# Feed layer of a four-stage transformer kernel: the first two attention tiles' scores, maxima and exponentials are issued among the last projected tiles

## The reference, cut to what matters

```
for l in range(2):                      # DEPTH
    h = shift_token(x)                  # 2048 tokens x 128 channels
    q, k, v = split(h @ wqkv)           # 8 heads x 64
    q, k = l2norm(q) * qs, l2norm(k) * ksc
    q, k = rotary_xpos(q, k)
    sim = 8.0 * q @ k                   # windows of 64, each with the one before it
    attn = softmax(where(mask, -max, sim))
    x = x + (attn @ v) @ wo
    h = layernorm(shift_token(x)) * lg + lb
    a, g = split(h @ w1 + b1)
    x = x + (a * gelu(g)) @ w2 + b2
```

## Time and profile before

| | |
|---|---|
| median of 3 runs | 1183.13 us (1181.82 to 1184.08) |
| the profiled execution | 1179.29 us, its span 1177.5 us |
| busy PE, DVE, ACT, POOL | 84%, 65%, 46%, 38% of the span |
| mean granted TensorE clock | 0.916 of full speed |
| feed loop and attention of layer 0 | about 766 to 939 us of the span |
| the same of layer 1 | about 968 to 1141 us of the span |

### The profile page before, as it was taken

How to read it: one execution, slowest core, us unless ns; L and a number is a source line. 1 busy time by engine, 2 the same in 40 slices (tenths; PEclk the granted TensorE clock), 3 DMA queues, 4 the chain that set the end, 5 groups by cost and what they waited for, 6 DMA issues and landing times.

```text
span 1177.5 us, 19933 instructions
## 1 busy us (share of the span) xinstructions
PE 990.9 (84%) x8002; PEld 661.3 (56%) x8002; DVE 762.8 (65%) x1340; ACT 537.3 (46%) x1243; POOL 452.9 (38%) x480
## 2 busy tenths in 40 slices
PE   5986997875479999999998568599698899979987
PEld 4645564744236787887877323245466534456643
DVE  7693585747556674554645888699566549946653
ACT  7745576462245423021120600067686436768632
POOL 7978106142025400000000345379454238934420
PEclk8977889987669999999999789799899999979999
DMA  3306818172428255236521100000121210012201
GB/s 109 73 1 120 148 25 148 26 132 55 166 109 153 45 108 131 53 107 108 94 57 71 60 1 0 0 1 1 37 55 38 72 52 27 1 38 55 56 1 36
DMA packets 60008, 75.58 MB, mean 64 GB/s; under 512 B 37460, under 2 KB 41952, under 8 KB 58188
## 3 DMA queue, kind: packets, MB, share of 16 engines
q1 hardware_dynamic: 59916, 74.31, 28.2%
HBM read 51.82 MB, written 1.51 MB: 45 GB/s over the span
## 4 chain that ended last, share of the span: by engine, by line
PE 56%; DVE 16%; POOL 15%; ACT 6%; issue 5%; DMA 1%; SPq 0%; POOLq 0%; DVEq 0%; ACTq 0%
PE psum L1630 7%; PE psum L1632 7%; PE psum L1631 7%; POOL rest L1909 3%; POOL rest L1899 3%; POOL rest L1905 3%; PE psum L2152 2%; PE psum L2145 2%; ACT rest L1843 2%; PE psum L2198 2%; PE psum L754 2%; POOL rest L1935 2%; DVE main L1999 2%; PE psum L2161 1%; PE psum L834 1%
## 5 line engine op out<-in xcount | busy, mean ns | idle before, releaser
L1843 ACT ACTIVATE rest<-psum,main 128x128 f32<-128x128 f32 x256 | 113.4, 480 | 11.4 <-POOL main L1920 8.9
L1349 POOL TENSOR_TENSOR kept<-kept 128x4 f32<-128x4 f32 x8 | 2.4, 303 | 295.2 <-DVE kept L1364 295.2
L1272 ACT ACTIVATE x_high<-main 128x512 fp32r<-128x512 f32 x48 | 30.4, 633 | 144.0 <-DVE main L1441 144.0
L1935 POOL TENSOR_TENSOR rest<-rest,main 128x512 f32<-128x512 f32 x64 | 65.4, 1044 | 45.5 <-DVE main L2005 45.5
L1630 PE MATMUL psum<-x_high,w_low 128*128 128x512 f32 x192 | 77.2, 402 | 0.7 <-DVE x_low L1446 0.7
L1630 PE MATMUL psum<-hid_high,w_low 128*128 128x512 f32 x192 | 75.8, 395 | 0.8 <-DVE main L1503 0.8
L1632 PE MATMUL psum<-x_high,w_high 128*128 128x512 f32 x192 | 75.8, 395 | 0.0
L1631 PE MATMUL psum<-x_low,w_high 128*128 128x512 f32 x192 | 75.7, 394 | 0.0
L1631 PE MATMUL psum<-hid_low,w_high 128*128 128x512 f32 x192 | 74.9, 390 | 0.0
L1632 PE MATMUL psum<-hid_high,w_high 128*128 128x512 f32 x192 | 74.8, 389 | 0.0
L1999 DVE TENSOR_REDUCE main<-psum 128x4 f32<-128x512 f32 x64 | 41.2, 686 | 40.5 <-PE psum L2145 40.4
(11 more groups left out here) (388 smaller groups left out, 2788.3 us busy)
## 6 DMA issues: line engine op xcount, KB each, us to landing
rest<-share_d SPq DMA_DIRECT2D x4, 3072.0 KB, 21.4
main<-main SPq DMA_DIRECT2D x32, 256.0 KB, 6.3
main<-k_pad SPq DMA_DIRECT2D x16, 512.0 KB, 8.0
rest<-share_d SPq DMA_DIRECT2D x4, 2048.0 KB, 16.9
rest<-main SPq DMA_DIRECT2D x32, 256.0 KB, 3.5
main<-w_dram SPq DMA_DIRECT2D x2, 3072.0 KB, 14.0
main<-rest SPq DMA_DIRECT2D x32, 128.0 KB, 2.3
rest<-tables_dram SPq DMA_DIRECT2D x2, 2048.0 KB, 8.7
```

The lines of the kernel that those rows point to most:

```text
L1843: last = A.activation(probs[:, p, 4 * r + m, :], bank[2 * p + r][:, m * P:(m + 1) * P], ACT.Exp, scale=row_scale[:, c, r, m:m + 1], bias=r ...
L1935: nc.gpsimd.tensor_tensor(probs[:, c % 2, four_heads], probs[:, c % 2, four_heads], row_sum[:, c % 2, four_heads].unsqueeze(2).to_broadcas ...
```

## The change

PE issues `score(0)` in round 16, ahead of the transposes of tile 14, and `score(1)` in round 17, ahead of those of tile 15. It waits there for the banks of tiles 14 and 15 (`ff_rot`, `ff_sq`, `ff_v`) and for the first two tiles of `qhT` and `khT`.

ACT copies the transposes of tile 14 ahead of the last root, takes the exponentials of tile 0 ahead of the copies of tile 15, and those of tile 1 behind them.

DVE takes `maxima(0)` ahead of the last inverse (round 16).

POOL makes `row_scale` of tiles 0 and 1 in round 3, that of the other 14 after the loop, and `bias(0)` ahead of the scaling of k of tile 15.

```
@@ ff_act
-                for c in range(TILES + 2):
+                def turned(c):
+                    for name, dst, bk in (("q", qhT, 4), ("k", khT, 5)):
+                        act.wait_ge(sem(f"ff_{name}T_ps"), L * TILES + c + 1)
+                        A.activation(dst[:, :, c * P:(c + 1) * P], bank[bk][:, :].rearrange("p (j t) -> p j t", j=4),
+                                     ACT.Copy).then_inc(sem(f"ff_{name}T"), 1)
+
+                for c in range(TILES + 1):
+                    if c == TILES:
+                        turned(c - 2)
...
+                    if 2 <= c < TILES:
+                        turned(c - 2)
...
                 exponentials(0)
+                turned(TILES - 1)
                 exponentials(1)
@@ ff_pool_layer
+            def scale_rows(tiles):
+                for r in range(2):
+                    last = nc.gpsimd.tensor_scalar(row_scale[:, tiles, r, :], inv_norm[:, tiles, 0, :].rearrange("p c (m r) -> p c r m", r=2)[:, :, r, :],
+                                                   QK_SCALE, None, ALU.mult)
+                chain.link(last)
...
+                if c == TILES:
+                    bias(0)
                 if c:
...
+                if c == 3:
+                    if L:
+                        pool.wait_ge(sem("at_exp"), L * 2 * TILES)
+                    scale_rows(slice(0, 2))
...
             pool.wait_ge(sem("ff_inv"), L * TILES + TILES)
-            bias(0)
+            scale_rows(slice(2, TILES))
             bias(1)
@@ ff_dve
                 for c in range(TILES + 1):
                     i = c % 2
+                    if c == TILES:
+                        maxima(0)
...
-                maxima(0)
                 maxima(1)
@@ ff_pe
+                    if c == TILES:
+                        for name in ("ff_rot", "ff_sq"):
+                            pe.wait_ge(sem(name), L * 2 * TILES + 2 * (TILES - 1))
+                        for name in ("ff_qT", "ff_kT"):
+                            pe.wait_ge(sem(name), L * TILES + 2)
+                        pe.wait_ge(sem("at_mask"), 1)
+                        score(0)
+                    if c == TILES + 1:
+                        for name in ("ff_rot", "ff_sq"):
+                            pe.wait_ge(sem(name), L * 2 * TILES + 2 * TILES - 1)
+                        pe.wait_ge(sem("ff_v"), L * TILES + TILES - 1)
+                        score(1)
...
-                score(0)
-                score(1)
```

More of the change, by code:

```diff
@@ L1894, in ff_pool_layer, with bias @@
         def ff_pool_layer(pool, chain, L):
+            def scale_rows(tiles):
[3 more added lines that the diff above has]
+                chain.link(last)
+            def bias(c):
+                pool.wait_ge(sem("at_max"), L * TILES + c + 1)
+                nc.gpsimd.tensor_tensor(row_bias[:, c % 2], neg_top[:, c % 2], row_scale[:, c], ALU.mult).then_inc(sem("at_bias"), 1)
             for c in range(TILES + 1):
@@ L1961, in ff_dve, with maxima @@
             for L in range(DEPTH):
+                def maxima(c):
+                    p = c % 2
+                    for r in range(2):
+                        dve.wait_ge(sem("at_s_ps"), L * 2 * TILES + 2 * c + r + 1)
+                        if c == 0:
+                            link(V.memset(bank[r][0:WINDOW, :].rearrange("p (m s) -> p m s", m=4)[:, :, 0:WINDOW], MASKED))
+                        last = V.tensor_reduce(neg_top[:, p, r], bank[2 * p + r][:, :].rearrange("p (m s) -> p m s", m=4),
+                                               AX.X, ALU.max, negate=True)
+                    last.then_inc(sem("at_max"), 1)
                 dve.wait_ge(sem("ff_tables"), L + 1)
@@ L1991, in ff_dve @@
                 dve.sem_inc(sem("ff_wqkv_free"), 1)
[L1993 to L2001, removed]
                 def inverse_sums(c):
@@ L2117, in project @@
                     T.matmul(bank[v][:, :], x, wqkv_sb[:, 1024:1536], start=True, stop=True).then_inc(sem("ff_v_ps"), 1)
[L2119 to L2130, removed]
                 def score(c):
@@ L2148, in score @@
                                     last.then_inc(sem("at_s_ps"), 1)
+                project(0)
+                for c in range(1, TILES + 2):
+                    if c < TILES:
+                        project(c)
+                    if c == TILES:
[10 more added lines that the diff above has]
+                        score(1)
+                    if c >= 2:
+                        for name, src, bk in (("q", q_rot, 4), ("k", k_rot, 5)):
+                            pe.wait_ge(sem("ff_" + name), L * TILES + c - 1)
+                            if c >= 3:
+                                pe.wait_ge(sem(f"ff_{name}T"), L * TILES + c - 2)
+                            for j in range(4):
+                                last = T.transpose(bank[bk][:, j * P:(j + 1) * P], src[:, (c - 2) % TURNED, j * P:(j + 1) * P], ident)
+                            last.then_inc(sem(f"ff_{name}T_ps"), 1)
                 def output(b):
@@ L2204, in ff_pe @@
                 pe.wait_ge(sem("ff_w_in"), L * 64 + 64)
-                pe.wait_ge(sem("at_mask"), 1)
-                score(0)
-                score(1)
                 for c in range(TILES + 1):
```

## The result

| | before | changed |
|---|---|---|
| median of 5 runs each | 1183.13 us (1180.38 to 1185.74) | 1173.07 us (1170.76 to 1176.07) |
| ratio of the runs, 95% interval | | 0.9919 (0.9892 to 0.9946) |
| profiled execution, its span | 1179.29 us, 1177.5 us | 1176.07 us, 1174.3 us |

The change made the kernel faster by 0.8%, 10.1 us between the medians, within the range of the prediction (1167.5 to 1175.0 us) and 2.2 us short of its 12.3. Yet the spans of the two profiled executions differ by only 3.2 us. The one of before, at 1179.29 us, is faster than all five runs of the table, and the one of the changed kernel, at 1176.07 us, is the slowest of its five. So the first question is where the executions part.

What follows compares the result with a forecast made beforehand. POOL was taken to set the feed loop's pace, followed by a hand-over in which almost nobody works. Starting score(2) 6.15 us earlier in each layer, 12.3 us together, gave 1183.13 - 12.3 = 1170.8 us, range 1167.5 to 1175.0.

Steps and rivals of the forecast that it cites:

- The scalings in round 3: POOL, feed loop: two 128 x 8 scalings and a wait delay everything behind by 0.45 us, bounds 0.35 and 0.87.
- score(0) and score(1) cost nothing: PE, rounds 16 and 17: score(0), 1.8 us, fills a 2.10 us gap; 2.5 us of slack cover score(1).
- maxima(0) and bias(0) are ready before ACT is: DVE and POOL, end of feed loop: tile 0's bias ready at 833.4 us, ahead of the set's load ending at 834.02.
- The load of the set on the path: ACT, behind the last root: the function set's load adds 1.28 us ahead of tile 0's exponentials, with no drain.
- Rival 3: ACT: the set's load has a tail of 1.4 us in each layer; gain 9.5 us, 1173.6 us; chance 0.06.
- The hand-over: From the end of the last floor to the start of score(2): some 6.3 us, where it was 12.9.
- The clock after the idle time: PE behind its idle time: score(2) and the transposes run as slowly as before, so score(2)'s end moves with its start.
- Rival 1: PE stays fast: score(2) takes 1.8 us, not 2.64 and 3.21; gain 14.5 us, 1168.6 us; chance 0.13.
- Rival 2: PE already slow at score(0), root 1.25 us late in each layer; gain 9.8 us, 1173.3 us; chance 0.07.
- The sum: Up to the start of score(2): 6.15 us gained in each layer, together 12.3 us.
- Rivals 4 and 5: Attention loop gives half the gain back, 1177.1 us (chance 0.08); feed loop falls out of step, 1186.4 us (0.03).
- rival 4: Attention loop: engines' phases shift and half the gain is lost, 6 us left, 1177.1 us; chance 0.08.

Runs made afterwards that it cites:

- e_act_scale: Changed kernel with row_scale of tiles 0 and 1 made on ACT in round 5, not POOL in round 3; first addition to end 391.88 us, changed 392.41.
- e_warm9: Changed kernel plus nine unused mask products on PE behind the last tile's transposes; first addition to end 389.95 us, changed 392.41.
- e_comb: Changed kernel with first two tiles' row scaling on ACT, last copies on DVE, seven unused PE products; median 1167.53 us, ratio to before 0.9879.
- e_dve_copy: Changed kernel with the last tile's two transpose copies on DVE behind maxima(1), not on ACT; first addition to end 391.65 us, changed 392.41.
- e_score1_late: Changed kernel with score(1) issued behind the transposes of tile 15, not ahead; first addition to end 394.28 us, changed 392.41.
- e_act_old: Changed kernel with ACT's copies of tile 15 ahead of both tiles' exponentials, not between them; first addition to end 397.40 us, changed 392.41.
- c_before: Control: the kernel before, run again with no edit; median 1181.30 us, ratio to before 0.9983, first addition to end 404.73 us.

## Why the prediction was right, point by point

- **What bounds.** Right. POOL has no gap in the feed loop, and the hand-over is ACT's chain from the last floor on.
- **The scalings in round 3.** The mechanism was right and the size was off: 0.45 us predicted, 0.75 and 0.71 us measured, within the bounds of 0.35 and 0.87. Each takes 0.24 us, little more than the 0.22 of the bias. What I had at nearly nothing were the gaps: 0.08 us ahead of the two, 0.07 between them and 0.08 behind them, where POOL waits for the last. e_act_scale shows that all of it came from POOL.
- **score(0) and score(1) cost nothing.** Right: score(0) took 1.76 us in a gap of 2.10, and the floor is released by POOL as before.
- **maxima(0) and bias(0) are ready before ACT is.** Right: the bias is done at 843.0 us, the load of the set ends at 843.7.
- **The load of the set on the path.** Right, 1.28 us and nothing behind it: the exponentials start 0.02 us later. Rival 3, the tail of 1.4 us that the Trainium skill states ("ScalarE: Activation LUTs", section "What ACT_TABLE_LOAD costs"), didn't show in any profile here: wherever the exponential's inputs were ready, it started within 0.02 us of the load's end.
- **The hand-over.** 6.3 us predicted from the end of the last floor to score(2), 6.26 or 6.27 us measured, in both layers and all three profiles of the changed kernel.
- **The clock after the idle time.** Right that the scores were slow, but the prediction also took score(2) to last as long as before, and in layer 0 it took 3.10 us, not 2.59. (Its sum for the scores at half rate, 1.19 + 1.96, borrows the 1.96 from the eight transposes; the 32 products of a tile's scores take 1.99 there, and the whole 3.1.) Rival 1, the fast scores, came true in no profile of the changed kernel; such scores were seen only where an edit was made, in e_warm9 and e_comb, and partly in e_dve_copy and e_score1_late. Rival 2 didn't happen, PE's clock was full at score(0).
- **The sum.** 6.15 us for each layer were predicted. By the parts: 6.65 us in each hand-over, less 0.75 and 0.71 us in the loop, less 0.5 us in score(2) of layer 0 (0.04 us gained in layer 1), and 0.65 and 0.54 us more from the rest of the layers, together 12.55 us against 12.3. The loop cost 0.56 us more than I had it and the slower score(2) 0.47 us, and the 1.2 us won behind score(2), for which I had nothing, make up for both. That is luck. From the end of score(2) to tile 7 nothing was won (31.2 us before and 31.3 now, in both layers); the 1.2 us lie behind tile 7, in the half that took 46.5 us in both layers before and 45.8 and 45.9 now, and why isn't known. Up to tile 7 the change had brought 11.2 us.
- **The time.** 1170.8 us predicted, 1173.07 us measured. The 95% interval of the ratio stands for a gain of 6.4 to 12.8 us and holds the predicted 12.3, so the difference may be chance. In the profiles no term of the sum is short by it; what differs there are the stages ahead of the change, which I had taken as fixed. Where the runs behind the median lost it can't be seen.
- **Rivals 4 and 5.** Nothing was given back in the attention loop of the changed kernel, and the later rounds of the feed loop kept their length. In the profiled execution of e_comb, 3.3 of 6 us were given back there, as rival 4 has it.

## What to carry to other kernels

At the border of two loops, ask for each first step of the second what it needs of the last steps of the first. Here it needed nothing of the last tiles, and the wait for all of them stood in front only because the code was written so; order on PE alone was worth nearly three quarters of the hand-over's gain, and, since it cost nothing in the loop, 10.4 of the 12.55 us of the whole.

What is moved into a loop is paid at the engine that sets its pace, with its wait; the same work was free on an engine that waits in each round. And when a reorder takes away a wait, look for what ran in its shade: the load of a function set and the copies here.

Read a gain from a point that the change can't have moved to the end, and only then from the whole time. Here that gave 12.0 to 13.5 us between any two of three profiles each, while the times gave 8 to 12. And stop reading where chance sets in again: up to tile 7 the parts of the changed kernel and its variants added up to within 0.3 us, and behind it they didn't.

## What the runs showed of the hardware that was not expected

- A load of ACT's function set stands right ahead of the first instruction that needs it. It doesn't wait for that instruction's semaphore (842.40 us, right behind the root), but it does stay behind everything ahead of it: in e_act_old it came only after the copies, 1.28 us on the path.
- Two scalings of 128 x 8 on POOL took 0.55 us, and delayed the next addition by 0.76 us. On ACT the two took 0.35 us, and the root behind them came no later.
- PE's clock in a given stretch differs between executions of the same program: in the kernel before, the same eight products took 3.71 us in c_before and 5.41 us in c_before2. Half of an attention loop that no kernel changed took 44.9 to 48.1 us over all kernels' profiles, and one and the same step of it ran at a granted clock of 0.50 in e_comb and 1.00 in the changed kernel.
